# Three LayerNorm applications of the last two chunks on ScalarE, with a GpSimd offset, in place of VectorE

## The reference

```python
x = layernorm(x + attention(x))           # 32 query heads of 8, 8 key/value heads, biases
x = layernorm(x + wkv_scan(w, u, x, ctx)) # running maximum, numerator, denominator over the tokens
x = layernorm(x + ffn(x))
# ffn(x) = layernorm(relu(x @ up_w)**2 @ down_w
#                    + (x @ expert_weight) * sum(top2(x @ gate_w))) * gamma + beta
# layernorm(h) = (h - mean) / sqrt(var + 1e-5), over the 256 channels
```

## Time and profile before

| | |
|---|---|
| median of 3 runs | 206.03 us (206.0 to 207.12) |
| the profiled execution | 205.89 us, its span 203.8 us |
| mean granted TensorE clock | 0.996 |
| busy in the span | PE 190.7, DVE 171.4, ACT 155.9, POOL 119.9 us |

### The profile page before, as it was taken

How to read it: one execution, slowest core, us unless ns; L and a number is a source line. 1 busy time by engine, 2 the same in 40 slices (tenths; PEclk the granted TensorE clock), 3 DMA queues, 4 the chain that set the end, 5 groups by cost and what they waited for, 6 DMA issues and landing times.

```text
span 203.8 us, 4423 instructions
## 1 busy us (share of the span) xinstructions
PE 190.7 (94%) x1311; PEld 112.3 (55%) x1311; DVE 171.4 (84%) x422; ACT 155.9 (76%) x344; POOL 119.9 (59%) x231
## 2 busy tenths in 40 slices
PE   7999999999998999999999999999999989999960
PEld 3744343344423345657474656854673677898940
DVE  7887977897999999799999899988968596876663
ACT  6741587878998989889899889989988974683630
POOL 8806356707557483564573848677499368365731
PEclk9999999999999999999999999999999999999998
DMA  6212623362120309000321020000030000000010
GB/s 212 97 51 57 238 58 84 79 225 61 50 68 26 87 8 326 8 24 0 79 67 45 2 61 0 8 3 8 26 84 3 0 0 27 3 2 27 26 51 26
DMA packets 13415, 11.76 MB, mean 58 GB/s; under 512 B 3664, under 2 KB 11344, under 8 KB 13136
## 3 DMA queue, kind: packets, MB, share of 16 engines
q1 hardware_dynamic: 13248, 11.35, 18.6%
q10 hardware_dynamic: 144, 0.13, 0.3%
HBM read 6.57 MB, written 1.05 MB: 37 GB/s over the span
## 4 chain that ended last, share of the span: by engine, by line
PE 68%; DVE 17%; issue 6%; ACT 4%; POOL 3%; POOLq 0%; DVEq 0%; ACTq 0%
PE ps_heads L693 11%; PE ps_max L664 9%; PE ps_b L855 8%; PE ps_b L872 7%; PE ps_exp L677 7%; DVE maxima L1287 7%; PE ps_a L813 4%; DVE top L1376 3%; PE ps_exp L855 3%; PE ps_b L838 2%; PE ps_a L767 2%; PE ps_a L756 2%; PE ps_heads L872 2%; PE ps_exp L705 2%; DVE den L1400 2%
## 5 line engine op out<-in xcount | busy, mean ns | idle before, releaser
L1287 DVE TENSOR_REDUCE maxima<-ps_max 128x2 f32<-128x512 f32 x128 | 82.1, 681 | 9.0 <-PE ps_max L664 8.5
L906 ACT ACTIVATE probs<-ps_exp 128x512 f32<-128x512 f32 x128 | 70.8, 596 | 10.1 <-PE ps_exp L677 9.5
L664 PE MATMUL ps_max<-k_rows,q_rows 64*128 64x256 bf16 x256 | 39.6, 272 | 1.6 <-DVE maxima L1287 1.1
L677 PE MATMUL ps_exp<-q_rows,k_rows 64*128 64x512 bf16 x128 | 37.9, 383 | 0.7 <-ACT probs L906 0.6
L693 PE MATMUL ps_heads<-probs,v_cols 128*32 128x512 f32 x256 | 33.9, 604 | 0.0
L1159 POOL TENSOR_TENSOR rstd<-var_eps,minus_half 128x1 f32<-128x1 f32 x32 | 18.7, 583 | 22.9 <-DVE var_eps L1252 22.8
L664 PEld LDWEIGHTS ps_max<-k_rows,q_rows 64*128 64x128 bf16 x256 | 14.7, 94 | 27.8 <-DVE maxima L1287 19.2
L872 PE MATMUL ps_b<-down_sb,inner_t 128*128 128x256 f32 x112 | 26.9, 381 | 0.0
L855 PE MATMUL ps_b<-x_t,up_sb 128*128 128x128 f32 x192 | 25.3, 279 | 0.6 <-DVE h L1476 0.4
L855 PEld LDWEIGHTS ps_b<-x_t,up_sb 128*128 128x128 f32 x192 | 23.1, 192 | 2.6 <-ACT relu_t L1041 1.3
L872 PEld LDWEIGHTS ps_b<-down_sb,inner_t 128*128 128x128 f32 x112 | 20.3, 190 | 2.7 <-issue 0.3
(11 more groups left out here) (153 smaller groups left out, 356.3 us busy)
## 6 DMA issues: line engine op xcount, KB each, us to landing
q_rows<-q_parts SPq DMA_DIRECT2D x42, 64.0 KB, 2.0
x_t<-in_x_cols SPq DMA_DIRECT2D x4, 256.0 KB, 3.9
x_in<-in_x SPq DMA_DIRECT2D x4, 256.0 KB, 2.9
ctx_t<-in_ctx_cols SPq DMA_DIRECT2D x4, 256.0 KB, 3.0
up_sb<-in_up_w SPq DMA_DIRECT2D x1, 1024.0 KB, 5.5
down_sb<-in_down_w SPq DMA_DIRECT2D x1, 1024.0 KB, 5.4
out_y<-y_out SPq DMA_DIRECT2D x8, 128.0 KB, 1.7
post_sb<-in_w_post SPq DMA_DIRECT2D x1, 906.0 KB, 5.5
```

What stands on the lines that cost most here:

```text
L664: last = nc.tensor.matmul(ps_max[n % 2][:, r, :], q_rows[b][at:at + HALF, g, REP * jj + 2 * half + r, h * P:h * P + P], k_rows[b][at:at + ...
L677: nc.tensor.matmul(ps_exp[n % 2][:, :], k_rows[b][at:at + HALF, JH * g + jj, kt * P:kt * P + P], q_rows[b][at:at + HALF, g, REP * jj:REP * ...
L906: nc.scalar.activation(probs[n % 8][:, :], ps_exp[n % 2][:, :], ACT.Exp, scale=SCALE).then_inc(s_exp, 1)
L1287: nc.vector.tensor_reduce(maxima[s % 2][:, g, j // JH, 0, at:at + 2], ps_max[n % 2][:, :, :], AX, ALU.max, negate=True).then_inc(s_max, 1)
```

## The change

The three norms 0, 1 and 3 of chunks 6 and 7 are done as those of the other chunks: VectorE adds a negated mean, GpSimd multiplies it by rstd, ScalarE applies rstd and offset. Norm 2 of these chunks stays as it was. The waits that VectorE's norms had stand in ScalarE's steps. The table of ticks isn't touched.

```diff
@@ ScalarE
-                    if AT["nor0"][p] == tick and p < WIDE:
+                    if AT["nor0"][p] == tick:
                         if before(p, 2):
                             a_done(act, ("yt", before(p, 2) - 1))
                         normalise(0, p, h1, x1[b % 2], s_x1[p >= WIDE])
...
-                    if AT["nor1"][p] == tick and p < WIDE:
+                    if AT["nor1"][p] == tick:
...
-                    if AT["nor3"][p] == tick and p < WIDE:
+                    if AT["nor3"][p] == tick:
@@ GpSimd
-                            if p < WIDE:
+                            if p < WIDE or k != 2:
                                 gp.wait_ge(s_negmean[k], p + 1)
                                 gp.wait_ge(s_rstd[k], p + 1)
                                 gp.tensor_tensor(offset[k][:, ti], neg_mean[k][:, ti], rstd[k][:, ti],
@@ VectorE
-                if p < WIDE:
+                if p < WIDE or k != 2:
                     nc.vector.tensor_scalar(neg_mean[k][:, ti], mean_var[k][:, ti, 0], -1.0, None,
                                             ALU.mult).then_inc(s_negmean[k], 1)
-
-            def normalise(k, p, src, dst, done):
-                dve.wait_ge(s_rstd[k], p + 1)
-                for i in CHUNKS[p][1]:
-                    last = nc.vector.tensor_scalar(dst[:, i, :], src[:, i, :], mean_var[k][:, i, 0:1],
-                                                   rstd[k][:, i:i + 1], ALU.subtract, ALU.mult)
-                last.then_inc(done, 1)
...
-                    if AT["nor0"][p] == tick and p >= WIDE:
-                        a_done(dve, ("yt", before(p, 2) - 1))
-                        normalise(0, p, h1, x1[b % 2], s_x1[p >= WIDE])
...
-                    if AT["nor1"][p] == tick and p >= WIDE:
-                        dve.wait_ge(s_x2b, before(p, 2))
-                        a_filled(dve, ("x2", before(p, 2) - 1))
-                        normalise(1, p, h2, x2[b % 2], s_x2[p >= WIDE])
...
-                    if AT["nor3"][p] == tick and p >= WIDE:
-                        stored(dve, before(p) - 1)
-                        normalise(3, p, h3, y_out, s_out[p >= WIDE])
```

## The result

The changed kernel's four launches took 209.28, 209.66, 210.38 and 212.91 us, a median of 210.02, against a median of 206.14 us before. So it is slower, and whether by less or more than 2% stays open; the forecast, 208.8 over 206.03, was 1.3%. The median of all four launches lies just above the forecast's range of 207.0 to 210.0, that of the other three, 209.66, inside it. The profiled execution took 209.66 us with a span of 207.6, 3.8 us more than before.

What follows compares the result with a forecast made beforehand. TensorE, busy 94% of the span, was taken as the bound, delayed by VectorE or ScalarE. 1.07 - 0.25 + 1.55 + 0.50 = +2.87 us on 205.89 gave 208.8 us, 8-in-10 range 207.0 to 210.0.

Steps and rivals of the forecast that it cites:

- Chunk 6, first norm: Tick 1116: the norm queues behind ScalarE exponentials, so TensorE's transposes of x1 start late; +1.07 us, bounds 0 and 1.3.
- rival a: One queue delay is absorbed: 207.7 us if chunk 6's 1.07 is, 207.2 if the square's delay doesn't bind; 20%.
- Chunk 6, second norm, VectorE's relief: Tick 1224: norm hidden on ScalarE, VectorE's scans start up to 0.30 us earlier; -0.25 us, bounds 0 and -0.38.
- Chunk 7, first norm: Tick 1217: hidden behind down-projection matmuls; 0.06 us counted because chunk 2's output norm moves behind it.
- Chunk 7, second norm: Tick 1290: chunk 6's second FFN square waits behind it on ScalarE, delaying TensorE's ninth down matmul; +1.55 us, bounds 1.4 and 1.8.
- The end: Third norms: chunk 6's hidden, chunk 7's the last computation before the last store; +0.50 us, bounds 0.3 and 0.7.
- Small additions: Six GpSimd multiplies already counted or in gaps, six VectorE negations hidden beside the power; 0.06 us allowed on the path.
- (b): Both queue delays are absorbed and only the ends remain: 206.1 us; 6%.
- (c): VectorE's queue sets the pace at chunks 6 and 7 and lost slots come back: -2.39 us, 203.5 us; 5%.
- (d): Holes in TensorE's work drop its clock to the 1.2 GHz level, doubling later matmuls at most: up to 218 us; 2%.
- (e): Something is dearer than counted, as a second wait in the order of chunk 7: 209.5 to 211 us; 9%.
- The rule of the Trainium skill: Gives 0.40 us per 256-element ScalarE norm where the rows say 0.60; the sum would be some 0.6 us smaller.

Runs made afterwards that it cites:

- e6: Changed kernel with chunk 6's first norm at tick 1111 for 1116, in front of two ScalarE exponentials; one time, 212.35 us, trace stretch 54.14 us (54.93 with the change).
- e4: Kernel before with only chunk 7's first and chunk 6's second norm moved to ScalarE; ratio 0.9992 (0.9952-1.0033).
- e9: Kernel before with GpSimd's sums x2 + beta of chunks 5 and 6 moved to ticks 1279 and 1291; ratio 0.9963 (0.992-1.0006).
- e10: e4 with GpSimd's sums x2 + beta of chunks 5 and 6 at the later ticks of e9; one time, 210.26 us, trace stretch 51.30 us.
- e5: Changed kernel with the square of chunk 6's second FFN half at tick 1289 for 1294, in front of chunk 7's second norm on ScalarE; ratio 1.007 (1.0021-1.0119).
- e12: The whole change again, unaltered, for more runs against the kernel before; ratio 1.0171 (1.0102-1.024), median 211.79 us, trace stretch 54.93 us.
- e1: Kernel before with only chunk 6's first norm (tick 1116) moved to ScalarE; ratio 1.004 (0.999-1.0089).
- e2: Kernel before with only chunk 7's second norm (tick 1290) moved to ScalarE; ratio 1.0091 (1.0045-1.0137).
- e3: Kernel before with only the two output norms of chunks 6 and 7 (ticks 1339, 1350) moved to ScalarE; ratio 0.9979 (0.9939-1.0019).

## Why the prediction was right, and by how much

- *Chunk 6, first norm.* Forecast +1.07, measured +1.18 alone and +1.16 in the whole; place, wait and mechanism as described, and e6 shows that the order made 0.8 of it. At the transposes it was 1.05 to 1.06; the rest is GpSimd's work beside VectorE's steps behind them, the cost for which the bound of 1.3 stood. No slack absorbed it (rival a), though the scans are shorter when they come later, as (a) had guessed.
- *Chunk 6, second norm, VectorE's relief.* This is the mis-sized term: -0.25 forecast, -0.03 measured. The earlier start came (0.31 us, 0.30 forecast), but I left GpSimd's sums where they stood. They had moved too and ran in one piece of 2.21 us right beside the scans, which took 1.56 us for 1.28. e4 has it alone, and e9 and e10 show what the sums cost: with them away there is still nothing to gain by moving the norm. It was the bound of 0 that I had kept.
- *Chunk 7, first norm.* Forecast hidden, and it was. The 0.06 us is not seen apart.
- *Chunk 7, second norm.* Forecast +1.55; alone 1.66. In the whole change 1.57 of it is the later start of the ninth down matmul (186.80 before, 190.00 less the 1.63 of shift after); the transposes behind come 0.97 us after that start, 0.88 before. e5 takes the wait away without touching the norm.
- *The end.* Forecast +0.50, measured +0.50.
- *Small additions.* Nothing found for the negations; the offset in front of GpSimd's sums is in the second point.
- *Sum.* 2.87 forecast, 3.29 measured in the stretch: 0.22 from the relief, 0.09 to 0.11 at each of the two queues. The profiled execution was 3.77 us over the one before; the further 0.48 to 0.53 lie ahead of h1 of chunk 6, where the change has no step yet.
- *Luck.* The forecast had no term for the spread of the start. In e12's series the same kernel's median, 211.79 us, is far above the range of 207.0 to 210.0; that the first series fell about its upper end is luck. The ratio is not: 1.013 forecast lies in both intervals.
- *The bounds.* Added to 205.89 us, the bounds given for the terms span 207.2 to 209.7, not 207.7 to 209.8; the range doesn't hang on it.
- *Rivals.* (b) and (c) fell with e1, e2 and e5: x1 was not written before 153.67, and ScalarE's later place decided. (d) fell with the row of clock 1.00. (e), something dearer, held in small: the relief that didn't come.
- *The rule of the Trainium skill* ("VectorE: DVE Perf Modes", section "The TRN2 errata": 224 cycles plus one for each element on ScalarE): the norms took 0.60 us after the change too, so the trace disagrees with it, and its 0.6 us smaller sum would have missed by more.

## What to carry to other kernels

In an order written out by hand, a step that changes engines keeps its tick but gets new neighbours: price it by what stands behind it in the new queue, in particular work that is ready when its own input isn't. Here that was 2.2 of 3.3 us, the slower engine and the extra offset at most 1.1. And before counting freed time on an engine, look at which shared work runs beside it then. Where executions differ by more than the effect, compare a stretch of the traces that starts behind the disturbance.

## What else the runs showed

**The start varies.** The first four matmuls of real data took 1.1 us in the execution before and 1.6 after. The groups by line from 4.0 to 6.5 us, of the kernel before and then of the kernel after (busy us, mean ns | idle before):

```profile
L756 PE MATMUL ps_a<-x_t,qk_sb 128*128 128x256 f32 x4 | 1.1, 398 | 0.0
```

```profile
L756 PE MATMUL ps_a<-x_t,qk_sb 128*128 128x256 f32 x4 | 1.6, 546 | 0.0
```

In the thirteen profiled executions this pair of numbers went from 1.03 to 2.04 us with no tie to the edit, and VectorE's first maximum from 10.7 to 12.0 us. That TensorE's clock rises later in some executions would fit. The trace's records of the granted clock begin at 4.23 us in the kernel before, where the four matmuls run from 4.34, and at 5.48 us in the kernel after, where they run from 4.44 to 6.05; in e4 and e6, the slowest at 2.04 us, they begin only behind these matmuls, at 6.62 and 7.02 us. For the time ahead of its first record no trace says what was granted, so the cause stays open.

**The clock fell in the middle of some executions.** In e6, e9, e10 and e12 the granted clock was at the 1.2 GHz level for a stretch from about 24 or 25 us on (in e10 near 15 us as well). TensorE had been busy for 3.67 of the 4 us from 20 to 24 us in e9; the kernel before, with 3.70, kept its clock, but so did the kernel after with the same 3.67. The stretch of e9, then that of the kernel before:

```profile
24.00:27.50 3.50, 3.50 (x17) 0.83 (x16) 1.77 (x5) 0.96 (x2) 0.00 (x0) 0.51 0.47 174
```

```profile
24.00:27.50 3.50, 3.50 (x23) 1.80 (x20) 2.95 (x6) 1.45 (x3) 1.13 (x3) 1.00 0.22 74
```

TensorE's instructions, matched one by one against the kernel before, came 1.4 to 1.5 us later across it in e6, e9 and e12, and 3.4 us across the two of e10. What set it off wasn't tried.

**Some late executions lose again later.** By the same matching, e4, e5, e6 and e12, which were 0.84 to 2.8 us late by 60 us, lost another 1.35 us near 75 us; those 0.75 late or less, as e3, didn't, and e9 and e10, 2.6 and 3.4 us late by then, didn't either. In e12 the waits from 66 to 82 us (total, times, longest) have one that the kernel before hasn't:

```profile
PEld ps_max L664 <- DMA q_rows<-q_parts: 1.0, 1, 1.0
```

So TensorE waited there for the copies of the queries' rows. Why these came late in some executions and not in others is open.
